# The first stage of a decoder layer kernel: mapping and biases loaded in rows and turned on TensorE, weights queued ahead of tables, first weights in halves, left-over values with 128 columns

## What is computed

```python
# self-attention: keys and values of 32 rows per segment of 128
qkv = (x @ Wqkv + bqkv)                      # x is normalised by row first
idx0 = mapping[segment * 128 + arange(0, 128, 4)]
Ksel, Vsel = k[:, :, idx0, :], v[:, :, idx0, :]
# cross-attention: all keys and values of the context, and one null row
kv = context @ Wkv                           # (2, 154, 1024) @ (1024, 2048)
k = concat(null_kv[0], k); v = concat(null_kv[1], v)
```

## Time and profile before

| | us |
|---|---|
| median of 3 runs | 1439.75 (1435.15 to 1444.11) |
| profiled execution, whole | 1451.07 |
| its span | 1449.4 |
| TensorE busy in the span | 1334.6 (92%) |
| VectorE, ScalarE, GpSimd busy | 931.5, 656.0, 399.0 |

### The profile page before, as it was taken

How to read it: one execution, slowest core, us unless ns; L and a number is a source line. 1 busy time by engine, 2 the same in 40 slices (tenths; PEclk the granted TensorE clock), 3 DMA queues, 4 the chain that set the end, 5 groups by cost and what they waited for, 6 DMA issues and landing times. The chain is left out here.

```text
span 1449.4 us, 31694 instructions
## 1 busy us (share of the span) xinstructions
PE 1334.6 (92%) x12420; PEld 1098.0 (76%) x12420; DVE 931.5 (64%) x1826; ACT 656.0 (45%) x1804; POOL 399.0 (28%) x475
## 2 busy tenths in 40 slices
PE   6998699999999969999999999999999886799998
PEld 5986477777777758788787887888888775587876
DVE  3526566666667556667776766777766676566563
ACT  3337232333333354555545455555554551455462
POOL 2200434344433101113112131131311113334442
PEclk9999799999999989999999999999999997899999
DMA  7545214222222210201102011020100301545430
GB/s 210 157 136 214 95 55 140 89 82 82 82 85 87 88 58 9 73 16 59 52 16 95 16 67 44 16 96 16 66 16 26 121 16 74 197 157 189 140 126 20
DMA packets 74389, 122.70 MB, mean 85 GB/s; under 512 B 18009, under 2 KB 26201, under 8 KB 74246
## 3 DMA queue, kind: packets, MB, share of 16 engines
q1 hardware_dynamic: 65926, 97.11, 20.5%
q0 software_dynamic: 8320, 23.62, 4.7%
HBM read 82.14 MB, written 42.07 MB: 86 GB/s over the span
## 5 line engine op out<-in xcount | busy, mean ns | idle before, releaser
L1304 ACT ACTIVATE b_prob<-bank,b_neg_top 128x155 f32<-128x155 f32 x496 | 186.7, 404 | 133.3 <-DVE b_neg_top L1444 123.9
L69 PE MATMUL bank<-turned_h,big_h 128*128 128x512 f32 x320 | 131.2, 410 | 4.4 <-PEq L99 2.9
L71 PE MATMUL bank<-turned_h,big_l 128*128 128x512 f32 x320 | 126.1, 394 | 0.0
L70 PE MATMUL bank<-turned_l,big_h 128*128 128x512 f32 x320 | 125.6, 393 | 0.0
L1709 PEld LDWEIGHTS bank<-ident,b_prob 128*128 128x128 f32 x640 | 95.3, 192 | 32.1 <-DVE b_pt L1461 14.1
L1709 PE MATMUL bank<-ident,b_prob 128*128 128x128 f32 x640 | 105.6, 289 | 12.8 <-DVE b_pt L1461 10.8
L1444 DVE TENSOR_REDUCE b_neg_top<-bank 128x6 f32<-128x930 f32 (+1 forms) x93 | 94.4, 1015 | 35.4 <-PE bank L1721 34.9
L69 PE MATMUL bank<-b_wo_h,b_ot_h 128*128 128x512 f32 x256 | 114.5, 447 | 0.4 <-DVE b_ot_l L1473 0.4
L1721 PE MATMUL bank<-k,wide 64*128 64x155 f32 x992 | 92.8, 316 | 14.6 <-ACT b_prob L1304 14.5
L71 PE MATMUL bank<-b_wo_h,b_ot_l 128*128 128x512 f32 x256 | 102.6, 401 | 0.0
L1304 ACT ACTIVATION_READ_ACCUMULATOR b_prob<-bank,b_neg_top 128x1 f32 x496 | 102.6, 207 | 0.0
(11 more groups left out here) (253 smaller groups left out, 3422.1 us busy)
## 6 DMA issues: line engine op xcount, KB each, us to landing
wide<-in_L_ffn_W_dram SPq DMA_DIRECT2D x16, 1024.0 KB, 5.3
slot_rows<-empty_row SPq DMA_DIRECT2D x1, 8256.0 KB, 24.5
raw<-in_L_xattn_Wkv_dram SPq DMA_DIRECT2D x8, 1024.0 KB, 5.9
a_xr<-in_x_dram SPq DMA_DIRECT2D x32, 256.0 KB, 2.6
x_scratch<-a_xr SPq DMA_DIRECT2D x32, 256.0 KB, 2.0
tiles<-x_scratch SPq DMA_DIRECT2D x32, 256.0 KB, 2.9
rows<-x_scratch SPq DMA_DIRECT2D x32, 256.0 KB, 3.0
out_dram<-rows SPq DMA_DIRECT2D x32, 256.0 KB, 2.0
```

The source lines that it names most:

```text
L69: pe.matmul(out, lh, rh, start=first, stop=False)
L70: pe.matmul(out, lh, rl, start=False, stop=False)
L71: return pe.matmul(out, ll, rh, start=False, stop=last)
L1304: last = act.activation(prob[:, n % 2, j, h:h + 2 * L2 - 1:2], s_banks[:, h, o:o + L2], ACT.Exp, bias=neg_top[:, n % 2, h, j:j + 1], accum ...
```

## The change

All of it is in `setup`.

- The mapping for the gathers is loaded as 4 rows of 512 entries (`map4`), cast to float on VectorE, and TensorE turns every fourth column into bank 7; VectorE adds the batch's offset into `kidx`. The mapping for the next stage's indices is loaded once as 16 rows of 128 (`map16`), the query and key biases and the null key as 9 rows (`cols`); all are turned behind block 0. `seg_raw` is loaded once instead of twice.
- SP's order is new: mapping, contexts, left-over context, first weights in two halves, small row loads, weights 1, `seg_raw`, weights 2, 3, biases, weights 4, biases, then weights 5 to 9 with the prefill between them, in 8 pieces, two behind each of the loads 5 to 8, then the null values, weights 10 and 11, and the transfers of `v_last`.
- The first split is done in halves, on ScalarE and VectorE, after all six context turns, and TensorE starts block 0 with the first half.
- Turns use four banks (0, 1, 5, 6). Left-over turns have 64 rows.
- `block_done` is gone: ScalarE waits on `kv_done`.
- For left-over values the low part of the left-over context stands in columns 64 to 127 beside the high part, so a group has 8 times 2 products (with high and low weights) instead of 8 times 3. The product low by low is in it now too. ScalarE copies rows 64 to 127 of the bank to `v_last`, and VectorE adds rows 0 to 63 (`rest_add`), behind its split of the next unit.
- GpSimd makes `ident` first. VectorE zeroes `ctx_rest`, and its memsets of `v2_rest` and `empty_row` come behind the first split.

The diff, cut to its core:

```diff
+            sp.dma_start(map4[:, :], mapping.rearrange("(n f) -> n f", n=4)).then_inc(keys_loaded, 16)
             for b in range(B):
                 sp.dma_start(ctx_sb[b], ctx[b, 0:P, :]).then_inc(ctx_loaded[b], 16)
-            load(0)
             sp.wait_ge(ctx_zeroed, 1)
             for b in range(B):
                 sp.dma_start(ctx_sb[2][32 * b:32 * b + REM, :], ctx[b, P:LC, :]).then_inc(ctx_loaded[2], 16)
...
+            for a in range(2):
+                sp.dma_start(raw[:, 0, 1024 * a:1024 * a + 1024].rearrange("p (k n) -> p k n", k=4),
+                             first[:, 4 * a:4 * a + 4, :]).then_inc(half_loaded if a == 0 else raw_loaded[0], 16)
+            sp.dma_start(map16[:, :], mapping.rearrange("(n p) -> n p", p=P)).then_inc(maps_loaded, 16)
+            sp.dma_start(cols[0:8, :], bqkv[0:2 * D].rearrange("(c p) -> c p", p=P)).then_inc(cols_loaded, 16)
...
             load(1)
...
+            load(2)
+            load(3)
...
+            for u in range(5, NC + 2):
                 load(u)
+                for a in range(2 * (u - 5), min(2 * (u - 5) + 2, 8)):
+                    prefill(a)
...
             def split(u):
                 if 2 <= u < NC + 2:
-                    act.wait_ge(block_done, u - 1)
+                    act.wait_ge(kv_done, ends[u - 2])
...
+            def rest_add(n):
+
+                dve.wait_ge(rest_copied, n - KB + 1)
+                part = v_last[0:64, (n - KB) * CB:(n - KB + 1) * CB]
+                dve.tensor_tensor(part, bank[2 + (ends[n] - 1) % 3][0:64, 0:CB], part, ALU.add).then_inc(rest_added, 1)
...
+            for u in range(2, NC + 2):
                 split(u)
+                if KB < u <= NC:
+                    rest_add(u - 1)
                 if u == XB:
                     norm(0)
                 if u == XB + 1:
...
                     norm(1)
...
             def turn(r, src):
-                need(pe, turned_low, r - 1)
+
+                need(pe, turned_low, r - 3)
...
-                        else:
+                        elif c < 2:
...
+                        else:
+                            for a in (wc_h, wc_l):
+                                last = pe.matmul(bank[2 + m % 3][:, 0:CB], ct_h[:, k, 2 * P:3 * P], a[:, n % 2, k, :],
+                                                 start=k == 0 and a is wc_h, stop=k == KC - 1 and a is wc_l)
                     last.then_inc(kv_done, 1)
                     m += 1
-                pe.wait_ge(kv_done, m)
-                pe.sem_inc(block_done, 1)
+                if n == 0:
+                    pe.wait_ge(maps_cast, 1)
+                    pe.wait_ge(cols_loaded, 48)
+                    pe.transpose(bank[7][:, 4:20], map16_f[:, :], ident[0:16, 0:16])
+                    pe.transpose(bank[7][:, 20:29], cols[:, :], ident[0:9, 0:9]).then_inc(tabs_turned, 1)
```

More of the change, by code:

```diff
@@ L254, in setup @@
     XB = 2
+    TURN_BANKS = (0, 1, 5, 6)
+    ends = [HB * min(n + 1, KB) + 3 * max(n + 1 - KB, 0) for n in range(NC)]
+    rests = [ends[n] - 1 for n in range(KB, NC)]
     block = nc.Block()
@@ L271, in _ @@
                 sp.dma_start(ctx_sb[2][32 * b:32 * b + REM, :], ctx[b, P:LC, :]).then_inc(ctx_loaded[2], 16)
[L272 to L279, removed]
@@ L280, in _ @@
-            load(1)
[L281 to L288, removed]
-                sp.dma_start(wr_sb[:, :, :], wr.rearrange("(k p) e -> p k e", p=P)).then_inc(biases_loaded, 16)
[L290 to L298, removed]
@@ L299, in _ @@
-            for u in range(2, NU):
+            first = units[0][0].rearrange("(k p) n -> p k n", p=P)
+            for a in range(2):
[3 more added lines that the diff above has]
+            sp.dma_start(cols[0:8, :], bqkv[0:2 * D].rearrange("(c p) -> c p", p=P)).then_inc(cols_loaded, 16)
@@ new lines, in _ @@
+            for s in range(2):
+                sp.dma_start(cols[8:9, s * D2:(s + 1) * D2], null_kv[0:1, :]).then_inc(cols_loaded, 16)
+            load(1)
+            with nc.allow_non_contiguous_dma(reason="one entry of a block's 64"):
+                sp.dma_start(seg_raw[0:1, :], mapping.rearrange("(a n f) -> a n f", a=1, f=BLK)[:, :, 0])\
+                    .then_inc(segs_loaded, 16)
+            load(2)
+            load(3)
+            sp.dma_start(bv_b[:, :], bqkv[2 * D:3 * D].partition_broadcast(P)).then_inc(biases_loaded, 16)
@@ L304, in _ @@
+            for u in range(NC + 2, NU):
+                load(u)
+            sp.wait_ge(rest_added, NC - KB)
             for b in range(B):
@@ L406, in _ @@
             split(NC + 1)
-            act.wait_ge(biases_loaded, 16 * 8)
+            act.wait_ge(biases_loaded, 16 * 6)
             for b in range(B):
@@ L467, in norm @@
                                       ALU.mult).then_inc(xk_norm, 1)
-            for r in range(4):
-                turn(r)
[L471 to L481, removed]
@@ new lines, in _ @@
+            dve.memset(ctx_sb[2][0:64, :], 0.0).then_inc(ctx_zeroed, 1)
+            dve.wait_ge(keys_loaded, 16)
+            dve.tensor_scalar(map4_f[:, :], map4[:, :], M - 1, None, ALU.min).then_inc(keys_cast, 1)
+            turn(0)
+            turn(1)
+            dve.wait_ge(keys_turned, 1)
+            for b in range(B):
+                last = dve.tensor_scalar(kidx[:, b, :], bank[7][:, 0:4], float(b * M), None, ALU.add)
+            last.then_inc(keys_placed, 1)
+            for r in range(2, CR):
+                turn(r)
@@ L487, in _ @@
+            for a in range(2):
+                first_split(a)
+            dve.wait_ge(maps_loaded, 16)
+            dve.tensor_scalar(map16_f[:, :], map16[:, :], M - 1, None, ALU.min).then_inc(maps_cast, 1)
+            dve.memset(v2_rest[:, :, :, :], 0.0).then_inc(zeroed, 1)
+            dve.memset(empty_row[:, :], 0.0).then_inc(empty_made, 1)
+            dve.wait_ge(empty_made, 1)
+            dve.memset(empty_row[:, D + 1:D + 2].bitcast(I32), NOBODY).then_inc(empty_made, 1)
             for e in range(E):
```

170 lines of the change are left out of this document (114 added, 56 removed).

## The result

The changed kernel takes 1421.76 us (median of 6 runs, 1420.55 to 1425.93) against 1437.27 of the kernel before (6 runs, 1435.1 to 1444.11): a ratio of 0.989, interval 0.9866 to 0.9915. Forecast were 1426.1 from a median of 1439.75, thus a gain of 13.6 us; measured are 15.5. The forecast left the gain just inside 1%, it lies just outside by its median, and the interval holds 1%, so on which side it lies can't be told.

The account below looks back on a forecast made before the run. The prediction took TensorE, busy in 92% of the span, as the bound. Its terms, -2.9 -3.7 -1.6 -1.1 -2.3 -3.8 +1.8, sum to -13.6 us, from a median of 1439.75 to 1426.1, range 1419 to 1434.

Parts of the forecast that it names:

- the gap with its fall of the clock: Before block 2: earlier load(2) removes TensorE's wait, -3.7 us, and the fall to the lower clock in block 2, -1.6.
- the block ends: Blocks 3 to 7: TensorE no longer waits for its own last product, five times 0.46 us, -2.3.
- the left-over products: Blocks 4 to 7: 16 products instead of 24 in the third group, 8 by 0.12 by 4, -3.8 us.
- the stall: Before block 6: VectorE's sum stands ahead of norm(1) and split(6), so TensorE waits, +1.8 us.
- splits that wait for raw in blocks 5 to 8: Sign against the forecast: ScalarE's splits waiting for raw weights in blocks 5 to 8 would show it wrong.
- The start: Before block 0: earlier left-over context, four banks and half splits let TensorE's products begin at 13.2 instead of 16.06, -2.9 us.
- The key turns: Between blocks 2 and 3: with four banks no turn waits for VectorE, 2.6 us instead of 3.73, -1.1.
- Because SP stood in seg_raw for 6.16 us and in eight v_rest issues for 7.10: Reason given for load(2)'s late issue at 26.43 and so the gap before block 2, whose removal was put at -3.7 us.
- load(7) and load(8) land 2 to 4 us before ScalarE can use them: Prefill pieces sharing the queue with weights, at 382 GB/s: no delay, costed at 0.
- weights a little late: Rival: behind the prefill, weights at 300 GB/s come 4.6 us late, 1430.7 us; chance 0.08.
- Start later: Rival: transfers, not VectorE, set the first product; gain 1.4 us instead of 2.9, 1427.6 us; chance 0.11.
- The clock in the stall: Rival: the clock falls in the 1.8 us stall before block 6, costing 1.6 us, 1427.7 us; chance 0.06.

Follow-up runs that it names:

- norm_first: The changed kernel with norm(1) ahead of the sum of block 4's left-over values on VectorE: median 1421.77 us, ratio 0.9882 to the kernel before.
- block_done_back: The changed kernel with TensorE's wait for its own last product and block_done restored at each block's end: 1422.43 us, run once.
- before_third: The kernel before, unchanged, profiled a third time, in the last set of runs: 1456.4 us.

## Why the forecast was right

Right were the walk and nearly all of its terms: the gap with its fall of the clock (-5.3 forecast, -5.3 in this pair of profiles), the block ends (0.46 each, and the undoing of six costs 2.9), the left-over products, the tail that doesn't change, the two transposes behind block 0 at 0, and the stall (+1.8 forecast, 1.7 found), which is also the one thing in the changed kernel that takes something back. Two reasons of the forecast were wrong, and its number survived them: the third and fourth point below. One of them is a sign by which the prediction called itself wrong, splits that wait for raw in blocks 5 to 8, and the changed kernel has such waits. That they cost nothing is luck, not insight.

- *The start* was mis-sized by 0.5: -2.9 forecast, -3.4 found. The walk put ScalarE's last turn at 10.8; it was done at 10.2, as its three last copies took 1.43 us.
- *The key turns* were mis-sized by 0.8: -1.1 forecast, -1.9 found. I took 16 transposes by 0.134, the pace of eight, and 0.45 for the changes of kind; they took 1.66 from first transpose to first product, and 0.15 ahead of them.
- *"Because SP stood in seg_raw for 6.16 us and in eight v_rest issues for 7.10"* is where the reasoning failed, though its number came out. Before, issue and data both held load(2): with the issue six us earlier and load(3) beside it, it landed at the same time. The changed kernel also moves the biases behind load(3) and starts the gathers 5.7 us sooner (10.72 instead of 16.45), and which of these was needed no run shows. The term is also no constant: 1.8 to 4.8 us of gap, with or without a fall, so that -5.3 came out to the tenth is luck of the pair of profiles.
- *"load(7) and load(8) land 2 to 4 us before ScalarE can use them"* was wrong. In the changed kernel ScalarE waits 1.51 and 0.64 us for them (0.43 for load(6), 1.41 for load(9)), and with the stall gone 2.27 and 3.16. I had them at 382 GB/s, and the stretch has 363, and the prefill pieces follow one another without a hole. They cost nothing only because the stall stands ahead of them. The rival "weights a little late" had the mechanism; its price was paid only in norm_first, and there it was 1.1 us, not 4.6.
- *Start later* did not come: the start was not set by landing. The Trainium skill (Perfetto Trace Analysis, DMA Optimizations) ties the gain of a split transfer to DMA engines that are otherwise idle. Here they were nearly full (share 0.95 from 4 to 8 us in the profile after), and the first half could still be used 1.2 us before the whole. The measurement decides: it helps here.
- *The clock in the stall* held, as in every pause of up to 2.2 us between products of the first stage, and it fell in those of 3.6 and 4.8. The length of one pause doesn't settle it, though. In the second stage of norm_first the granted clock fell behind a pause of 1.58 us, and in the third stage of the changed kernel behind one of 1.17 (at 860.28, to 0.55 on the mean of the window 860 to 863). That the stall kept the clock was thus less safe than the rival's two rows made it look.

That the median gain (15.5) is a little above the forecast agrees with the two terms above (1.3 us) and is within the interval's width (some 3.5 us each way). The time itself, 1421.76, lies 4.3 under the forecast, and 2.5 of that are the median before, which was 1439.75 by three runs and is 1437.27 by six. One can't say more from whole times: first stages of the kernel before differ by 5 us among three profiles.

## What to carry to other kernels

Before two profiles are compared, cut both at a barrier that the change doesn't move: half of the 30 us between these two lay in a stage that was the same code. A transfer that is late by its issue can be late by its data too, and then taking away one alone can bring nothing; look at the share of the DMA engines between issue and landing. And a cost that shows as 0 because a stall stands ahead of it comes back with the stall's removal, so the two have to be tried together.

## What was not expected of the hardware

- 2048 products of 32x64 in the second stage took 28.8 us with 0.9 of idle time in some sets of runs (up to 3.0 of idle time in two profiles), and 34.3 with 9.1 in others, 8.1 of it "issue", with either kernel. Whole times of the kernel before were 1434 to 1445 in the first set and 1445 to 1456 in the last, which had another chip.
- Block 0, which starts at TensorE's lower clock (steps of 0.27 us for 320 columns, then of 0.15), took 8.9 to 10.5 us to block 1's start in profiles of kernels that have the same products there (8.93 in norm_first, 9.48 in the changed kernel, 10.50 in block_done_back with 0.3 us of its own wait). The slow steps last 3.3 us in norm_first, 4.6 in the changed kernel, 6.0 in block_done_back and 6.3 in before_third. When the clock rises after the first product thus differs by 3 us between executions. The PEclk column reads 1.00 in the first 17 us of the changed kernel, beside these slow steps, so the pace is the measure there.
